# Graph attention in a four-layer network: the 0/1 matrices are compared on VectorE instead of GpSimd

## The chip, the cores and the metric

One core of a Trainium2 chip runs the whole program. The metric is the time of one execution on the device, in microseconds (us); lower is better. A measured time is the median of several executions. The profile is of one further execution and gives every instruction's start and duration.

## The reference, cut to what matters

Four layers follow each other: graph attention (GAT), a mixture-of-experts layer, a three-hop graph layer and a recurrent layer. The change touches only the attention over the edges of the first one: 6250 nodes with 256 features each, 100,000 edges sorted by destination, 4 heads of 64 channels.

```python
e = a_src[src] + a_dst[dst]                      # per edge and head
e = jnp.where(e > 0, e, NEG_SLOPE * e)
m = jax.ops.segment_max(e, dst, num_segments=n)
p = jnp.exp(e - m[dst])
denom = jax.ops.segment_sum(p, dst, num_segments=n)
alpha = p / jnp.maximum(denom[dst], 1e-16)
msg = alpha[:, :, None] * h_src[src]
out = jax.ops.segment_sum(msg, dst, num_segments=n).reshape(n, HC) + bias
```

## The kernel before, in words

The sorted edges lie in 832 tiles of 128 edges, and a tile's edges all end in one block of 128 destination nodes. `gat_attend` works through them in 104 groups of U = 8 tiles. For every tile a 128 x 128 matrix of zeros and ones says which edge (partition) ends in which node of the block (column). It is made by comparing a row of column numbers, `k.cols`, with each edge's place in the block, `local`. The fp32 matrix `S` multiplies the messages `M` on TensorE, which sums them per node (`product`, L1068). The bf16 copy `Sb` is used to find a running maximum (`spread_out`, L1037 and L1040) and is turned over on TensorE (`turn`, L1047).

Each engine runs its own list of instructions and waits on counters (semaphores). All lists are written in steps; step n has the end of group n and earlier stages of the groups n + 1, n + 2 and n + 3:

- GpSimd (POOL) compares the eight tiles of a group (`build`, L1001, eight instructions that write fp32 `S`), then issues the eight gathers that fetch rows of `table` for the group after it (`fetch`, L1007). Those are indirect DMAs into `G` (called all_X in the profile, since it lies in the room of X).
- ScalarE (ACT) takes the indices (`index`, L936 and L937), computes a correction (L962), copies part of the gathered rows (`collect`, L945), takes the turned matrices (`take_turned`, L954), casts `S` to bf16 (`halve`, L941), exponentiates (`weigh`, L958), scales the gathered rows of four tiles (`messages`, L968, 16 instructions), and last copies what the next step's `spread_out` multiplies (`sources`, AT, L949).
- TensorE (PE) goes through u = 0..7. It has `spread_out` for u = 0 and 1, then `ask` (L1055, L1057), `product` 0, `spread_out` 2, `turn`, `product` 1, `spread_out` 3, `product` 2 and so on. Here `spread_out` u may start only when VectorE has reduced `spread_out` u - 2 (counter `topped`), because two PSUM banks take turns.
- VectorE (DVE) begins a step with `bases` (L1166, L1167), two `message` instructions (L1209), with L1170 and L1173 between and behind them. Then come `reduce[0]` and `reduce[1]` (L1120, maxima of what `spread_out` made), `scale` (L1180), `into[0]` (L1220, adds `product` 0 to the sums), `whole` (L1189), `reduce[2]`, `into[1]` and so on up to `into[7]`. The small instructions for the logits lie between them; the last of those, `guard` (L1204), releases `weigh`. A chain for the maxima ends the step (L1136 to L1154). At every even step VectorE first loads 16 block numbers into registers (`blocks_of`), at the price of an idle engine before L1166.

What follows one step ahead of another on an engine is decided by this written order alone; nothing is scheduled by a tool.

Of the kernel before, what the change touches and what calls it, by code (L numbers as in the profile page):

```python
# [6 lines left out]
BF16 = mybir.dt.bfloat16  # L7
I32 = mybir.dt.int32
ACT = mybir.ActivationFunctionType
ALU = mybir.AluOpType  # L10
AXX = mybir.AxisListType.X

P = 128
# [13 lines left out]
U = 8  # L27
# [839 lines left out]
def gat_attend(nc, k, table, order, SRT, tile_block, QT, bigi, acc, room):  # L867
# [3 lines left out]
    with Phase(nc, "gs") as ph:  # L871
# [7 lines left out]
        local = ph.sb("local", [P, NS, U])  # L879
# [28 lines left out]
        indexed, turns, built, halved = ph.sem("indexed"), ph.sem("turns"), ph.sem("built"), ph.sem("halved")  # L908
# [18 lines left out]
        with ph.block() as block:  # L927
# [6 lines left out]
            def _(act):  # L934
# [4 lines left out]
                def halve(n, r):  # L939
                    act.wait_ge(built, n + 1)  # L940
                    nc.scalar.copy(Sb[:, r % 2], S[:, r]).then_inc(halved, 1)  # L941
# [30 lines left out]
                def step(n, r, i, there):  # L972
                    if there(0):
                        act.wait_ge(carried, (U - LATE) * (n + 1))
                        act.wait_ge(msgs, NPART * (n + 1))
                    if there(0) and there(4):
                        index(n + 4, r)
                    if there(0):
                        correct(n)
                    if there(3):  # L980
                        collect(n + 3, (r + 3) % NS, i + 1 if r else i)
                    if there(2):
                        take_turned(n + 2)
                    if there(3):
                        halve(n + 3, (r + 3) % NS)
                    if there(1):
                        weigh(n + 1, r + 1)
                        messages(n + 1, (r + 1) % NS)
                    if there(3):
                        sources(n + 3, (r + 3) % NS)  # L990
# [6 lines left out]
            def _(pool):  # L997
                def build(n, r):
                    pool.sem_inc(turns)
                    for u in range(U):  # L1000
                        last = nc.gpsimd.tensor_scalar(S[:, r, u], k.cols[:], local[:, r, u:u + 1], None, ALU.is_equal)  # L1001
                    last.then_inc(built, 1)

# [7 lines left out]
                for n in range(NS):  # L1011
                    pool.wait_ge(indexed, n + 1)
                    if n < 3:
                        build(n, n)
                    fetch(n, n)
                with pool.Fori(1, QUADS) as i:
                    for r in range(NS):
                        n = NS * i + r
                        pool.wait_ge(indexed, n + 1)
                        build(n - 1, (r - 1) % NS)  # L1020
                        fetch(n, r)
                pool.wait_ge(msgs, NPART * (GROUPS - NS + 1))
                build(GROUPS - 1, NS - 1)

            @block.tensor
            def _(pe):
# [4 lines left out]
                def spread_out(n, r, u):  # L1031
                    if u == 0:
                        pe.wait_ge(halved, n + 1)
                        pe.wait_ge(acopied, n + 1)
# [26 lines left out]
                def product(n, r, u):  # L1061
                    if u < LATE:
                        pe.wait_ge(msgs, n * NPART + next(j for j, (a, z) in enumerate(PARTS) if a <= u < z) + 1)
                    else:
                        pe.wait_ge(carried, n * (U - LATE) + u - LATE + 1)
# [33 lines left out]
            def _(dve):  # L1099
# [5 lines left out]
                ch.mark(nc.vector.tensor_copy(eye[:], k.ident[:]))  # L1105
                ch.mark(nc.vector.reduce_sum(picks[:], k.ident[0:TA, 0:TA].rearrange("p (u j h) -> p u h j", u=U, j=TERMS), AXX))
# [9 lines left out]
                dve.sem_inc(ready, 1)  # L1116

# [106 lines left out]
                def step(n, r, i, there):  # L1224
# [14 lines left out]
                    for j in range(1, NPART):  # L1239
                        if there(0):  # L1240
                            message(r, j)
                        if j == 1:
                            apart()
                    reduce[0]()
# [1330 lines left out]
```

## Time and profile before

| | |
|---|---|
| median of 3 executions | 17562.97 us |
| lowest and highest | 17558.74 and 17570.36 us |
| profiled execution, first to last instruction | 17545.4 us |
| the attention's edge part, `gat_attend` | 1254 to 2852 us of it, 1598 us |
| VectorE, GpSimd, TensorE, ScalarE busy in that part | 1329.62, 1312.56, 1204.22, 732.83 us |
| granted TensorE clock there, share of full speed | 0.80 |

The profiled execution's span is 17.6 us less than the median of the timed ones, which also hold what lies before the first and behind the last instruction. Busy time is a union over an engine's instructions. The edge part is 9% of the span; the recurrent layer, from about 7500 us on, is most of the rest.

### The profile page before, as it was taken

Reading aid. Unit: us, or ns where it says so; the run is one execution under the profiler, and the core shown is the slowest. Engines: PE = TensorE matmul, PEld = TensorE weight load, DVE = VectorE, ACT = ScalarE, POOL = GpSimd, SP = SyncE. Lnnn points to the kernel's source line nnn. Section 1 sums busy time; section 2 is a strip of 40 time slices with the busy share of each in tenths; the row PEclk is TensorE's granted clock in tenths of the full one; section 3 lists DMA queues with packets and bytes.
Section 4 is the critical chain, followed back from the end, with each engine's and each line's share of the span. In section 5 each row is a group of like instructions: output and inputs, shape, how many; then the busy total and the mean of one; then the engine's idle time right before and its main releaser. Section 6 shows DMA issues by size and latency. Waiting matters only on the chain. (4 is left out here: it accounts for less than half of the span.)

```text
span 17545.4 us, 683245 instructions
## 1 busy us (share of the span) xinstructions
PE 12730.7 (73%) x250869; PEld 10213.3 (58%) x250870; DVE 11697.3 (67%) x68713; ACT 5986.8 (34%) x41949; POOL 5631.1 (32%) x6174
## 2 busy tenths in 40 slices
PE   5247773399655656556888888888888888888887
PEld 3135552266444544445777777777777777777776
DVE  7368887322555454556777777777777777777777
ACT  0004442011100101003555555554555555555555
POOL 4778887666576575772000000000000000000000
PEclk6558886599877777775555555555555555555555
DMA  0102222111333333331000000000000000000000
GB/s 22 25 21 73 74 72 43 56 34 33 101 105 98 96 105 87 105 105 37 4 4 4 4 4 4 4 4 4 4 4 4 4 4 4 4 4 4 4 4 18
DMA packets 352412, 609.44 MB, mean 35 GB/s; under 512 B 157501, under 2 KB 232222, under 8 KB 348988
## 3 DMA queue, kind: packets, MB, share of 16 engines
q0 software_dynamic: 223104, 471.33, 10.4%
q1 hardware_dynamic: 126524, 100.27, 1.9%
q8 instruction: 1835, 30.06, 0.7%
q14 instruction: 949, 7.77, 0.1%
HBM read 508.72 MB, written 62.45 MB: 33 GB/s over the span
## 5 line engine op out<-in xcount | busy, mean ns | idle before, releaser
L2402 PE MATMUL lr_ZI<-ls_h,ls_V 128*128 128x1 f16 x150000 | 5006.8, 166 | 1669.7 <-DVE ls_h L2451 1412.8
L2402 PEld LDWEIGHTS lr_ZI<-ls_h,ls_V 128*128 128x128 f16 x150000 | 4487.3, 104 | 2677.0 <-DVE ls_h L2451 2640.4
L2419 ACT ACTIVATE ls_tg<-lr_ZI 128x2 f32<-128x2 f32 x12500 | 2150.0, 172 | 4626.5 <-PE lr_ZI L2402 4534.6
L2446 DVE TENSOR_TENSOR_SCAN lr_c<-ls_tg,ls_one_hc 128x2 f32<-128x2 f32 x12500 | 2118.1, 170 | 1441.0 <-ACT ls_tg L2419 1317.8
L2358 POOL COPY ls_HT<-ls_h 128x250 f32 x50 | 19.8, 395 | 9358.3 <-DVE ls_h L2456 9358.3
L2402 PE MATMUL lr_ZO<-ls_h,ls_V 128*128 128x1 f16 x75000 | 2865.0, 165 | 0.0
L671 PE MATMUL prop_sum<-prop_G,prop_S 128*128 128x256 f32 x4992 | 1830.4, 546 | 1369.9 <-DMA prop_G<-hop_table,prop_idx 1369.9
L657 POOL DMA_INDIRECT prop_G<-hop_table,prop_idx x2496 | 2368.3, 949 | 1057.3 <-issue 708.8
L2402 PEld LDWEIGHTS lr_ZO<-ls_h,ls_V 128*128 128x128 f16 x75000 | 2483.2, 104 | 0.0
L671 PEld LDWEIGHTS prop_sum<-prop_G,prop_S 128*128 128x128 f32 x4992 | 1403.9, 288 | 1796.3 <-issue 1486.1
L2451 DVE TENSOR_TENSOR ls_h<-ls_to 128x1 f16<-128x1 f32 x12500 | 2023.4, 162 | 479.1 <-ACT ls_to L2424 16.0
L2424 ACT ACTIVATE ls_to<-lr_c 128x1 f32<-128x1 f32 x12500 | 2102.5, 169 | 9.9 <-DVE lr_c L2446 1.0
L2422 ACT ACTIVATE ls_to<-lr_ZO 128x1 f32<-128x1 f32 x12500 | 2069.3, 171 | 0.0
L2455 DVE TENSOR_TENSOR_SCAN ls_h<-ls_to,ls_h 128x2 f16<-128x2 f32 x12500 | 1633.5, 162 | 25.7 <-issue 25.7
L694 DVE TENSOR_TENSOR gnn_agg<-gnn_agg,prop_sum 128x256 f32 x1664 | 694.9, 418 | 908.7 <-PE prop_sum L671 884.9
L2458 DVE TENSOR_TENSOR ls_one_hc<-ls_h,lr_c 128x1 f32<-128x1 f32 x6250 | 969.0, 155 | 220.0
L633 ACT CAST prop_idx<-gnn_SRT 128x8 int32 (+1 forms) x312 | 63.3, 203 | 2915.2 <-DMA prop_G<-hop_table,prop_idx 2903.7
L680 DVE TENSOR_SCALAR prop_S<-all_cols,prop_lw 128x128 f32<-128x128 f32 x2520 | 900.5, 358 | 165.6 <-issue 153.3
L2456 DVE TENSOR_TENSOR ls_h<-ls_to 128x2 f32<-128x2 f32 x6250 | 952.9, 152 | 7.2 <-issue 7.2
L2459 DVE TENSOR_TENSOR ls_one_hc<-ls_h,lr_c 128x1 f32<-128x1 f32 x6250 | 930.2, 149 | 0.0
L522 POOL DMA_INDIRECT sd_records<-sc_rec,sc_place x784 | 772.5, 985 | 440.7 <-issue 408.0
L1007 POOL DMA_INDIRECT all_X<-gat_table,gs_idx x832 | 825.3, 992 | 239.1 <-issue 239.1
(455 smaller groups left out, 13965.7 us busy)
## 6 DMA issues: line engine op xcount, KB each, us to landing
prop_G<-hop_table,prop_idx POOLq DMA_INDIRECT x2496, 2.7
mow_W<-in_L_ffn_W SPq DMA_DIRECT2D x16, 1024.0 KB, 10.8
moe_out<-me_Ys SPq DMA_DIRECT2D x108, 128.0 KB, 1.7
all_X<-gat_table,gs_idx POOLq DMA_INDIRECT x832, 2.8
hop_table<-ht_T SPq DMA_DIRECT2D x50, 256.0 KB, 2.1
sd_records<-sc_rec,sc_place POOLq DMA_INDIRECT x784
ss_records<-me_recs,me_places POOLq DMA_INDIRECT x540
gat_table<-gt_hs SPq DMA_DIRECT2D x50, 128.0 KB, 1.8
```

The costliest lines, as they stand in the source:

```text
L657: nc.gpsimd.indirect_dma_start(out=G[:, r, u, :], out_offset=None, in_=table[:, :], in_offset=bass.IndirectOffsetOnAxis(ap=idx[:, r, u:u + ...
L671: nc.tensor.matmul(ps[u][:, 0:D], S[:, r % 2, u, :], G[:, r, u, :], start=True, stop=True).then_inc(mm, 1)
L2402: mm = nc.tensor.matmul(place(hf, bank, col, 1), (V2 if part == "21" else V1)[:, q, ROWS.index(row), :], hx[:, prev, q, 1:2], start=False, ...
L2419: nc.scalar.activation(tg[:, s % 2, m, :], place(hf, m, col, 2), ACT.Tanh, scale=back).then_inc(gates[m], 1)
L2422: nc.scalar.activation(to[:, s % 2, m, 1:2], place(hf, KD + m, col, 1), ACT.Sigmoid, scale=back)
L2424: nc.scalar.activation(to[:, s % 2, m, 0:1], c[m][:, 1:2], ACT.Tanh, scale=0.5).then_inc(tanh_made[m], 1)
L2446: nc.vector.tensor_tensor_scan(c[m][:, 0:2], tg[:, e, m, :], one_hc[:, m, :], 1.0, ALU.mult, ALU.add).then_inc(cell[m], 1)
L2451: nc.vector.tensor_tensor(h1[:, r, m, 1:2], to[:, e, m, 1:2], to[:, e, m, 0:1], ALU.mult).then_inc(h1_made[m], 1)
L2455: nc.vector.tensor_tensor_scan(h2[:, r, m, :], to[:, e, m, :], h1[:, r, m, :], 1.0, ALU.mult, ALU.subtract).then_inc(h2_made[m], 1)
L2456: nc.vector.tensor_tensor(h[:, r, :], to[:, e, :, 1], to[:, e, :, 0], ALU.mult).then_inc(h_made, 1)
L2458: nc.vector.tensor_tensor(one_hc[:, 0, 1:2], h[:, r, 0:1], c[0][:, 1:2], ALU.mult)
L2459: nc.vector.tensor_tensor(one_hc[:, 1, 1:2], h[:, r, 1:2], c[1][:, 1:2], ALU.mult).then_inc(hc_made, 1)
```

## The change

`build` leaves GpSimd. VectorE now compares a whole group, 8 x 128 columns, with one `tensor_tensor` that reads bf16 column numbers and bf16 `local` and writes `Sb`. ScalarE's `halve` (fp32 to bf16) becomes `widen` (bf16 to fp32), of the same 1024 columns. The new VectorE instruction stands in step n for group n + 3, between `apart` (L1173) and `reduce[0]`. On ScalarE `take_turned` now comes ahead of `collect`. GpSimd keeps only the gathers.

```diff
-        local = ph.sb("local", [P, NS, U])
+        local, cols = ph.sb("local", [P, NS, U], BF16), ph.sb("cols", [P, P], BF16)
...
-                def halve(n, r):
+                def widen(n, r):
                     act.wait_ge(built, n + 1)
-                    nc.scalar.copy(Sb[:, r % 2], S[:, r]).then_inc(halved, 1)
+                    nc.scalar.copy(S[:, r], Sb[:, r % 2]).then_inc(widened, 1)
...
-                    if there(3):
-                        collect(n + 3, (r + 3) % NS, i + 1 if r else i)
                     if there(2):
                         take_turned(n + 2)
                     if there(3):
-                        halve(n + 3, (r + 3) % NS)
+                        collect(n + 3, (r + 3) % NS, i + 1 if r else i)
+                        widen(n + 3, (r + 3) % NS)
...
-                def build(n, r):
-                    pool.sem_inc(turns)
-                    for u in range(U):
-                        last = nc.gpsimd.tensor_scalar(S[:, r, u], k.cols[:], local[:, r, u:u + 1], None, ALU.is_equal)
-                    last.then_inc(built, 1)
-
...
                     for r in range(NS):
                         n = NS * i + r
                         pool.wait_ge(indexed, n + 1)
-                        build(n - 1, (r - 1) % NS)
                         fetch(n, r)
-                pool.wait_ge(msgs, NPART * (GROUPS - NS + 1))
-                build(GROUPS - 1, NS - 1)
...
                     if u == 0:
-                        pe.wait_ge(halved, n + 1)
+                        pe.wait_ge(built, n + 1)
                         pe.wait_ge(acopied, n + 1)
...
                 def product(n, r, u):
+                    if u == 0:
+                        pe.wait_ge(widened, n + 1)
...
+                def build(n, r, first):
+                    dve.wait_ge(indexed, n + 1)
+                    if not first:
+                        dve.wait_ge(widened, n - 1)
+                    nc.vector.tensor_tensor(Sb[:, r % 2], cols[:].unsqueeze(1).broadcast_to([P, U, P]),
+                                            local[:, r].unsqueeze(2).broadcast_to([P, U, P]), ALU.is_equal).then_inc(built, 1)
...
                         if j == 1:
                             apart()
+                    if there(3):
+                        build(n + 3, (r + 3) % NS, not there(1))
                     reduce[0]()
                     reduce[1]()
```

On VectorE this is the place in the middle of the steps, before the change; gs_gap is `apart`, gs_top the reductions, gat_acc `scale` and `into`.

```order
L1209 TENSOR_TENSOR gs_M<-all_X,gs_M 128x8x64
L52 REGISTER_ALU
L1173 TENSOR_TENSOR gs_gap<-gs_pair 128x4 [waits gs_pairs]
L1119 ISA
L1120 TENSOR_REDUCE gs_top<-gs_M 128x4 [waits gs_spread]
L1119 REGISTER_ALU
L1120 TENSOR_REDUCE gs_top<-gs_M 128x4 [waits gs_spread]
L1178 ISA [waits gs_corrected]
L1180 ISA [waits gs_added]
L1180 TENSOR_TENSOR gat_acc<-gat_acc,gs_corr 128x260
L1220 TENSOR_TENSOR gat_acc<-gat_acc,gs_O 128x260 [waits gs_scaled,gs_mm]
```

And this is the same place in the changed kernel, whose lines there have numbers that are lower by one or two.

```order
L1207 TENSOR_TENSOR gs_M<-all_X,gs_M 128x8x64
L52 REGISTER_ALU
L1171 TENSOR_TENSOR gs_gap<-gs_pair 128x4 [waits gs_pairs]
L1110 REGISTER_ALU
L1113 TENSOR_TENSOR gs_Sb<-gs_cols,gs_local 128x1024 [waits gs_widened,gs_indexed]
L1117 ISA
L1118 TENSOR_REDUCE gs_top<-gs_M 128x4 [waits gs_spread]
L1117 REGISTER_ALU
L1118 TENSOR_REDUCE gs_top<-gs_M 128x4 [waits gs_spread]
L1176 ISA [waits gs_corrected]
```

One instruction of 1024 columns, with waits on `widened` and `indexed`, has come between the messages and the first reduction.

On ScalarE this piece of the difference stands in the middle of the steps; hops0 is the counter of a group's gathers, gs_ST the turned matrices.

```order
 L937 COPY gs_idx<-edges_SRT 128x8
 L962 ACTIVATE gs_corr<-gs_gap 128x4 [waits gs_paired]
-L944 ISA
-L945 COPY gs_GA<-all_X 128x96 [waits hops0]
 L953 ISA
 L954 CAST gs_ST<-gs_T 128x512 [waits gs_trans]
 L953 REGISTER_ALU
 L954 CAST gs_ST<-gs_T 128x512 [waits gs_trans]
-L941 CAST gs_Sb<-gs_S 128x1024 [waits gs_built]
+L944 ISA
+L945 COPY gs_GA<-all_X 128x96 [waits hops0]
+L941 CAST gs_S<-gs_Sb 128x1024 [waits gs_built]
```

The copy that waits for the gathers has moved behind the two casts, and the cast of 1024 columns has turned round.

## Rows read from the trace of the kernel before

**Rows 1.** The page: the span.

```profile
span 17545.4 us, 683245 instructions
```

**Rows 2.** Windows, cut at every second step's L1166: busy time, clock, DMA.

```profile
core 0: us, PE busy (x) PEld busy (x) DVE busy (x) ACT busy (x) POOL busy (x), PEclk, DMA share, GB/s
1996.80:2025.50 28.70, 20.99 (x158) 13.88 (x155) 25.02 (x75) 14.05 (x50) 24.14 (x32) 0.87 0.28 72
2025.50:2055.40 29.90, 23.69 (x173) 16.09 (x172) 25.19 (x75) 14.08 (x50) 25.16 (x33) 0.78 0.28 75
...
sum 119.40, PE 92.39 PEld 61.98 DVE 100.72 ACT 56.35 POOL 100.78; mean PE 23.10 PEld 15.49 DVE 25.18 ACT 14.09 POOL 25.20
```

**Rows 3.** Groups by line, 1320 to 2820 us: busy, mean ns, idle before, releasers.

```profile
L1007 POOL DMA_INDIRECT all_X<-gat_table,gs_idx x798 | 790.4, 990 | 229.3 <-issue 229.3
L1001 POOL TENSOR_SCALAR gs_S<-all_cols,gs_local 128x128 f32<-128x128 f32 x800 | 468.0, 600 | 3.6 <-ACT gs_idx L937 0.5
...
L1220 DVE TENSOR_TENSOR gat_acc<-gat_acc,gs_O 128x260 f32 x804 | 334.6, 416 | 125.3 <-PE gs_O L1068 118.6
...
L1209 DVE TENSOR_TENSOR gs_M<-all_X,gs_M 128x512 f32<-128x512 f32 x202 | 138.0, 685 | 0.0
...
L941 ACT CAST gs_Sb<-gs_S 128x1024 bf16<-128x1024 f32 x100 | 104.6, 1046 | 155.7 <-POOL gs_S L1001 155.6
...
L1166 DVE TENSOR_TENSOR gs_pair<-gs_mine,gat_QT 128x4 f32<-128x4 f32 x101 | 16.4, 162 | 70.1 <-issue 70.1
```

**Rows 4.** Timeline of step 48: start, duration, instruction, [idle before, releaser].

```profile
2026.43 1.21 PE L1068 MATMUL gs_O<-gs_M,gs_S 128*128 128x260 f32 x2
...
2026.99 1.27 DVE L1120 TENSOR_REDUCE gs_top<-gs_M 128x4 f32<-128x512 f32 x2
...
2027.72 0.61 PE L1037 MATMUL gs_M<-gs_bigs,gs_Sb 128*128 128x512 bf16 x1
...
2029.40 1.18 PE L1068 MATMUL gs_O<-gs_M,gs_S 128*128 128x260 f32 x2
...
2030.73 0.42 DVE L1220 TENSOR_TENSOR gat_acc<-gat_acc,gs_O 128x260 f32 x1 [0.73 <-PE gs_O L1068]
...
2034.91 0.17 DVE L1204 TENSOR_SCALAR gs_e<-gs_e 128x32 f32<-128x32 f32 x1
```

**Rows 5.** Timeline of step 49, the next one.

```profile
2040.99 1.33 DVE L1120 TENSOR_REDUCE gs_top<-gs_M 128x4 f32<-128x512 f32 x2
...
2041.86 1.22 PE L1068 MATMUL gs_O<-gs_M,gs_S 128*128 128x260 f32 x2
...
2042.86 0.63 PE L1037 MATMUL gs_M<-gs_bigs,gs_Sb 128*128 128x512 bf16 x1
...
2043.11 0.42 DVE L1220 TENSOR_TENSOR gat_acc<-gat_acc,gs_O 128x260 f32 x1 [0.45 <-PE gs_O L1068]
...
2045.90 0.43 DVE L1220 TENSOR_TENSOR gat_acc<-gat_acc,gs_O 128x260 f32 x1 [1.25 <-PE gs_O L1068]
```

**Rows 6.** Timeline of step 47.

```profile
2011.67 1.28 DVE L1120 TENSOR_REDUCE gs_top<-gs_M 128x4 f32<-128x512 f32 x2
...
2012.81 0.63 PE L1037 MATMUL gs_M<-gs_bigs,gs_Sb 128*128 128x512 bf16 x1
```

**Rows 7.** Groups by line and shape on VectorE, 0 to 2900 us.

```profile
L247 DVE TENSOR_TENSOR ss_oh<-ssb_bins,ss_binrow 128x400 bf16<-128x400 f32 x197 | 108.9, 573 | 71.5 <-DVE ss_pos L343 29.9 <-PEq L251 29.1 <-PE ss_cnt L306 11.1
...
L1309 DVE TENSOR_TENSOR gf_XL<-gat_acc,gf_den 128x3200 f32<-128x3200 f32 x4 | 13.7, 3485 | 0.0
...
L1109 DVE CAST gs_pick<-gs_picks 96x4096 bf16<-96x4096 f32 x1 | 2.3, 2290 | 0.0
```

**Rows 8.** Timeline of the first steps.

```profile
1254.78 4.67 POOL L1001 TENSOR_SCALAR gs_S<-all_cols,gs_local 128x128 f32<-128x128 f32 x8 [12.54 <-ACT gs_idx L937]
...
1288.38 0.27 ACT L945 COPY gs_GA<-all_X 128x96 bf16<-128x96 bf16 x1 [13.93 <-DMA all_X<-gat_table,gs_idx]
...
1303.04 0.27 ACT L945 COPY gs_GA<-all_X 128x96 bf16<-128x96 bf16 x1 [12.31 <-DMA all_X<-gat_table,gs_idx]
```

More of the change, by code:

```diff
@@ L907, in gat_attend @@
         ready, primed, listed, mapped = ph.sem("ready"), ph.sem("primed"), ph.sem("listed"), ph.sem("mapped")
-        indexed, turns, built, halved = ph.sem("indexed"), ph.sem("turns"), ph.sem("built"), ph.sem("halved")
+        indexed, turns, built, widened = ph.sem("indexed"), ph.sem("turns"), ph.sem("built"), ph.sem("widened")
         collected, aturned, acopied, spread, topped = ph.sem("collected"), ph.sem("aturned"), ph.sem("acopied"), ph.sem("spread"), ph.sem("topped")
@@ L1012, in _ @@
                     pool.wait_ge(indexed, n + 1)
-                    if n < 3:
-                        build(n, n)
                     fetch(n, n)
@@ L1105, in _ @@
                 ch.mark(nc.vector.tensor_copy(eye[:], k.ident[:]))
+                ch.mark(nc.vector.tensor_copy(cols[:], k.cols[:]))
                 ch.mark(nc.vector.reduce_sum(picks[:], k.ident[0:TA, 0:TA].rearrange("p (u j h) -> p u h j", u=U, j=TERMS), AXX))
```

## The prediction, made before the changed kernel ran

> **What bounds the kernel now.** I read the edge part step by step, since nothing else changes. First the windows: eight steps take 119.4 us, 14.93 us each, and no engine is full; GpSimd and VectorE are both busy for 12.6 us of a step [rows 2]. Then the groups by line. GpSimd spends 8 x 0.60 us on compares and 8 x (0.99 + 0.29) us on gathers, the 0.29 being the "issue" idle of 229.3 us over 798 of them: 4.8 + 10.2 = 15.0 us, all of a step. It waits for nobody [rows 3]. So GpSimd looks like the bound, and a change that takes a third of its work away looks like a clear gain.
>
> VectorE's idle time argues against that. It is 2.3 us a step (14.93 - 12.59) [rows 2]: 1.25 us before L1220, nearly all for TensorE's products, and 0.70 us before L1166, which is the loading of block numbers and belongs to the engine itself [rows 3]. None of it is a wait for GpSimd. The only one who waits for a compare is ScalarE's cast L941, 1.56 us a step, and ScalarE is busy for only 7.0 us of a step [rows 2, 3]. So GpSimd keeps pace with the others but seldom holds them. The loop that sets the step runs through VectorE and TensorE: reduction 0 frees a PSUM bank, `spread_out` 2 fills it, then come `turn` and `product` 1, and `into[1]` waits for that. In step 48 reduction 0 ends at about 2027.6 (two take 1.27 us), `spread_out` 2 starts at 2027.72, `product` 1 at 2029.40, and VectorE, which was there 0.73 us early, goes on at 2030.73 [rows 4].
>
> **The change, part by part.**
>
> *GpSimd* loses 4.8 us a step. Nobody but ScalarE's cast sees it, so I price it at nothing in the steady state. Its gathers start as soon as the indices are there, which is when the messages are made (ahead of reduction 0, 1.5 us into step 48), and are through 10.2 us later. The copy that wants them comes in the next step. If GpSimd did hold the loop, this would be worth what the second rival below says.
>
> *VectorE gains one compare of 1024 columns a step.* No row has it. From 512 to 3200 columns two-input instructions go from 685 to 3485 ns, 1.04 ns a column, so 1024 columns take 685 + 512 x 1.04 = 1.22 us; 400 columns compared in the same way, with one value repeated along the row, take 573 ns and lie on that line [rows 3, 7]. The next instruction starts some 0.08 us before such a record ends (in step 48 two reductions of 0.68 us make 1.27), so it costs the engine 1.15 us. From below: a cast of 4096 columns takes 2290 ns, 0.56 ns a column, half as long [rows 7]; at that pace the compare costs 0.6 us. I take 1.15 us, because the row of 573 ns is the same operation, in the same layout, though with fp32 inputs.
>
> The Trainium skill's "VectorE: DVE Perf Modes", § Rules for kernel authors, says that tensor_tensor in bf16 gets twice the rate; its "Vector Engine (DVE) Microarchitecture Reference", § 5.1 Performance modes, says that one element read again and again in a two-source op of 2-byte operands ran at the single rate. No row here has such an instruction. By estimates from these pages the compare would cost 0.6 us by the first and 1.15 by the second.
>
> *How much of it lands on the loop.* The compare stands right ahead of reduction 0, so everything that hangs on reduction 0 moves back by 1.15 us, unless TensorE was late anyway.
> - Even steps (48): `product` 0 ends at 2027.64 and reduction 0 at about 2027.6; TensorE is ready when the bank is. With the compare, `spread_out` 2 starts at about 2028.8, and `into[1]` moves by the same: +1.05 us. Its wait of 0.73 us hides nothing, since it hangs on the same reduction [rows 4].
> - Odd steps (49): TensorE begins later there, because VectorE has no numbers to load first; `product` 0 ends at 2043.08, reduction 0 already at about 2041.65. `spread_out` 2 at 2042.86 is 1.2 us behind the reduction. The compare fits in, and the waits of 0.45 and 1.25 us shrink instead: +0.0 us [rows 5].
> - Odd steps with a fast start (47): reduction 0 at about 2012.3, `spread_out` 2 at 2012.81, so 0.5 us is covered and +0.65 us is left [rows 6].
>
> Of four pairs of steps one is like (46, 47), and three are like (48, 49). The mean is ((1.05 + 0.65) + 3 x (1.05 + 0)) / 8 = 0.61 us a step.
>
> *The granted clock.* The pair 46 and 47 has 0.87 of full speed and takes 28.7 us, the other three have 0.77 to 0.78 and take (119.4 - 28.7) / 3 = 30.2 us [rows 2]. TensorE now idles about 1 us more per even step. If the fast pairs vanish, a pair costs 30.2 + 1.05 = 31.3 us, 15.64 us a step, +0.71. I take 0.65 us, between the two.
>
> *ScalarE.* `widen` casts as many columns as `halve`, 1.05 us, and has nothing to wait for: the compare is through at about 2.7 us of a step (1.5 + 1.15), and ScalarE reaches the cast after `take_turned`. What must not wait is `weigh`, behind `guard`, and that ends at 2035.1, 9.6 us into step 48 [rows 4]; about 6 us lie between for 2.5 us of copies. `collect` moves behind `take_turned`; TensorE wants it only after `spread_out` 5. Nothing is charged. The new waits of VectorE (`indexed`, `widened`) are for things that were done a step before.
>
> *The start.* The second and third `collect` wait 13.9 and 12.3 us for gathers, at 1288.38 and 1303.04, because GpSimd compares ahead of each [rows 8]. Without the three compares of 4.7 us the gathers come 4.7, 9.4 and 14 us earlier. The reductions and the chains of these steps then set the pace; I take 10 us saved of 14. In the last three steps there is no compare, and nothing changes.
>
> **The sum** against the profiled execution's own 17545.4 us [rows 1]: 101 steps x 0.65 = +66, less 10, is +56 us. The median of the runs shown is 17.6 us above that span and takes the same difference: 17563 + 56 = 17619 us.
>
> **The rivals.**
>
> *1. GpSimd is the bound after all (faster).* For it: it never pauses. If its cadence is what makes TensorE late, the waits for products go with it. A step is then VectorE's 12.59 + 0.70 + about 0.15 + 1.15 = 14.6 us, 0.33 less than now: 101 x -0.33 - 10 = -43 us, 17520. It decides once the wait before L1220 falls from 1.25 to under 0.6 us a step. Against it: that wait hangs on reduction 0 in the timeline, and the compare comes ahead of that. Chance 0.12.
>
> *2. Little is left of it (no change).* Either the compare runs at the rate of the cast: even steps +0.5, odd ones 0, 101 x 0.25 - 10 = +15 us, 17578. That has 0.07. Or all pairs become as fast as the first: 28.7 + 1.7 = 30.4 us a pair, 15.2 us a step, 101 x 0.27 - 10 = +17 us, 17580. With the pairs that end in between, that has 0.15.
>
> *3. Full price (slower still).* The clock sinks further or the slack of the odd steps is used up, and each step takes the whole 1.15 us: 101 x 1.15 - 10 = +106 us, 17669. The same direction has a collision: VectorE's compare reads two operands in SBUF while GpSimd's gathers run. Today L1209 does that in each step and its mean is 685 ns, on the line of the others, so VectorE loses nothing that shows. If each compare waited out a whole gather of 0.99 us [rows 3], half of that landing on the loop, it would be +50 us on top of the forecast, 17669 too. Chance 0.12 together, 0.03 of it the collision.
>
> The Trainium skill's "SBUF — State Buffer" calls the port pair that VectorE and GpSimd share an exclusive lock, held for the whole instruction, and counts a VectorE op with two SBUF inputs against a GpSimd op that reads SBUF. By that rule the collision would be there; the rows of L1209 do not show it.
>
> **How the numbers follow.** The forecast, +40 to +80 us, has 0.54, and the rivals 0.12, 0.22 and 0.12. A measurement of this kernel tells about 0.2%, 35 us, from no change. Faster by more holds rival 1: 0.12. Slower by more holds the forecast and rival 3, less a little for forecasts that come out low: 0.64. The rest is 0.24. For 8 in 10 the range takes in rivals 2 and 3, with 20 us beyond the latter for its rough size, and stops short of rival 1's 17520: 17535 to 17690 us. The forecast's own range is 17600 to 17645.
>
> **What would show it.** In the profile after: a compare of about 1.22 us (0.69 would be the fast rate); GpSimd at about 10 us a step; ScalarE no longer waiting for gathers; even steps near 15.1 us and odd ones near 16, pairs of 31 us; the idle before L1220 still near 1 us a step; the first full step about 10 us earlier. The forecast is wrong if pairs of steps fall under 29.5 us, which is rival 1, or if the odd steps grow as much as the even ones, which is rival 3.

## The result, and the profile after

The changed kernel takes 17614.52 us (median of 7 executions, 17610.99 to 17618.51). The kernel before, run beside it on the same chip, takes 17560.69 us (7 executions, 17555.98 to 17570.36). The ratio is 1.003, with a 95% interval of 1.0019 to 1.004: 0.3%, or 54 us, slower. The prediction said 17619 us, and 17535 to 17690 as its range.

The page's span after, against [rows 1]:

```profile
span 17609.2 us, 682620 instructions
```

The edge part in one window, 1254 to 2912 us (it ends at 2909; before it ended at 2852):

```profile
core 0: us, PE busy (x) PEld busy (x) DVE busy (x) ACT busy (x) POOL busy (x), PEclk, DMA share, GB/s
1254.00:2912.00 1658.00, 1223.14 (x8424) 812.39 (x8424) 1437.60 (x3965) 725.18 (x2601) 794.78 (x832) 0.77 0.27 69
```

GpSimd went from 1312.56 busy us to 794.78, VectorE from 1329.62 to 1437.60. TensorE's granted clock is 0.77 of full speed where it was 0.80. Four steps (48 to 51), two windows cut at every second step's L1164, which is the L1166 of before:

```profile
2048.30:2078.81 30.51, 22.28 (x152) 14.79 (x151) 27.19 (x76) 13.87 (x50) 15.27 (x16) 0.78 0.27 71
2078.81:2109.97 31.16, 23.48 (x180) 15.88 (x177) 27.28 (x77) 13.95 (x50) 15.17 (x16) 0.78 0.27 70
```

Each pair holds about 2 us more of VectorE than before [rows 2]. Before, pairs of steps took 29.9, 30.6, 30.2 and 28.7 us by turns, and the last kind had a granted clock of 0.87 to 0.88 against 0.77 to 0.78 (twice 0.83) in the others. After, the pairs take 30.3 to 31.7 us and none has more than 0.78: the fast pair is gone. Over groups 10 to 100 the mean step went from 14.95 to 15.63 us: even steps from 14.01 to 15.14, odd ones from 15.88 to 16.12. That is +0.68 us a step.

Groups by line in the edge part, 1320 to 2880 us (columns as in [rows 3]; L1000 is the old L1007, L1218 the old L1220, L1207 the old L1209, L1164 the old L1166):

```profile
L1000 POOL DMA_INDIRECT all_X<-gat_table,gs_idx x789 | 750.6, 951 | 787.6 <-ACT gs_idx L937 564.5 <-issue 223.1
...
L1218 DVE TENSOR_TENSOR gat_acc<-gat_acc,gs_O 128x260 f32 x799 | 335.4, 420 | 93.0 <-PE gs_O L1058 81.7
...
L1207 DVE TENSOR_TENSOR gs_M<-all_X,gs_M 128x512 f32<-128x512 f32 x200 | 136.5, 686 | 0.0
L1113 DVE TENSOR_TENSOR gs_Sb<-gs_cols,gs_local 128x1024 bf16<-128x1024 bf16 x99 | 120.9, 1221 | 0.0
...
L941 ACT CAST gs_S<-gs_Sb 128x1024 f32<-128x1024 bf16 x99 | 104.6, 1057 | 0.0
...
L958 ACT ACTIVATE gs_M<-gs_e 128x32 f32<-128x32 f32 x100 | 26.0, 260 | 348.3 <-DVE gs_e L1202 348.3
...
L1164 DVE TENSOR_TENSOR gs_pair<-gs_mine,gat_QT 128x4 f32<-128x4 f32 x100 | 16.4, 164 | 70.1 <-issue 70.1
```

GpSimd, which never paused, now waits 5.6 us a step for the next indices. ScalarE's wait for GpSimd's compares, 155.7 us before L941, is gone, and so is its wait for gathers, 343.5 us before `collect`. This is `collect` in the kernel before, 1320 to 2820 us:

```profile
L945 ACT COPY gs_GA<-all_X 128x96 bf16<-128x96 bf16 x100 | 27.1, 271 | 343.5 <-DMA all_X<-gat_table,gs_idx 343.5
```

In their place ScalarE waits 348.3 us for VectorE's last logits (L1202), where it waited 51.5. VectorE still spends nearly 1 us a step before L1218 waiting for products. So the engine that was relieved is idle, and what the others wait for goes back to VectorE and TensorE. ScalarE is part of that loop: TensorE waits 2.9 us a step for its copy `sources` (L949) at the start of a step, and waited 3.0 before.

The timeline of step 48, an even one, shows the price on the path (columns as in [rows 4]):

```profile
2048.30 0.16 DVE L1164 TENSOR_TENSOR gs_pair<-gs_mine,gat_QT 128x4 f32<-128x4 f32 x1 [1.65 <-issue]
...
2049.80 1.22 DVE L1113 TENSOR_TENSOR gs_Sb<-gs_cols,gs_local 128x1024 bf16<-128x1024 bf16 x1
...
2050.94 1.28 DVE L1118 TENSOR_REDUCE gs_top<-gs_M 128x4 f32<-128x512 f32 x2
...
2051.68 0.10 PEld L1025 LDWEIGHTS gs_M<-gs_bigs,gs_Sb 128*128 128x128 bf16 x1 [1.99 <-DVE gs_top L1118]
2051.68 0.61 PE L1025 MATMUL gs_M<-gs_bigs,gs_Sb 128*128 128x512 bf16 x1 [1.25 <-DVE gs_top L1118]
...
2053.36 1.18 PE L1058 MATMUL gs_O<-gs_M,gs_S 128*128 128x260 f32 x2
...
2054.70 0.42 DVE L1218 TENSOR_TENSOR gat_acc<-gat_acc,gs_O 128x260 f32 x1 [0.74 <-PE gs_O L1058]
```

The reader is to see the two waits in the middle. TensorE stands 1.25 us idle until the first reduction (L1118) gives the bank back; in step 48 of the kernel before it had no wait there [rows 4]. Then L1218, which is `into[1]`, waits 0.74 us for the product, as it waited 0.73 before [rows 4]. The whole chain has moved. And step 49, an odd one:

```profile
2064.59 1.22 DVE L1113 TENSOR_TENSOR gs_Sb<-gs_cols,gs_local 128x1024 bf16<-128x1024 bf16 x1
...
2065.73 1.28 DVE L1118 TENSOR_REDUCE gs_top<-gs_M 128x4 f32<-128x512 f32 x2
...
2066.47 0.10 PEld L1025 LDWEIGHTS gs_M<-gs_bigs,gs_Sb 128*128 128x128 bf16 x1 [0.53 <-DVE gs_top L1118]
2066.47 0.63 PE L1025 MATMUL gs_M<-gs_bigs,gs_Sb 128*128 128x512 bf16 x1
...
2069.36 0.43 DVE L1218 TENSOR_TENSOR gat_acc<-gat_acc,gs_O 128x260 f32 x1 [0.61 <-PE gs_O L1058]
```

Here `into[1]` starts 6.3 us into the step (2069.36 less 2063.09), as before (6.4), and its wait has shrunk from 1.25 to 0.61 us [rows 5]: the compare took the place of waiting.

### The profile page after: what moved, and what is told of

Same layout as the page of the kernel before. It is cut to its first block and busy times, and to the rows that moved or that the text cites. A ratio compares the mean times of both kernels' runs of the same rounds, so it can differ in the third digit from the quotient of the medians.

```text
span 17609.2 us, 682620 instructions
## 1 busy us (share of the span) xinstructions
PE 12741.8 (72%) x250869; PEld 10217.3 (58%) x250870; DVE 11833.5 (67%) x68818; ACT 5988.7 (34%) x41949; POOL 5111.5 (29%) x5342
## 5 line engine op out<-in xcount | busy, mean ns | idle before, releaser
L1000 POOL DMA_INDIRECT all_X<-gat_table,gs_idx x832 | 794.8, 955 | 820.0 <-ACT gs_idx L937 570.5
```

## The experiments

The chips on which these ran take 19,400 to 19,600 us for the kernel before, not 17,560: what lies ahead of the recurrent layer is longer there (the edge part begins at about 1880 us instead of 1254), and in the steps of the edge part VectorE, TensorE and ScalarE stand idle for 2 to 4 us at a time. Runs with the same letter (e, f, g, h) ran on the same chip, beside the same runs of the kernel before. Each is compared with those, and totals of different chips are not set side by side. No variant was timed on a chip like the first. What does carry over is the time of an instruction after the start of its step, read before any of those idle stretches: for the kernel before `into[1]` of an even step starts at +5.26 us on the first chip and on these.

| run | us | before, same chip | ratio (95% interval) | mean step | `into[1]`, even and odd step |
|---|---|---|---|---|---|
| e1_relief_alone | 19589.41 | 19423.92 | 1.0084 (1.0065 to 1.0102) | 19.74 | +5.26, +5.40 |
| e2_gpsimd_load_back | 19738.61 | 19423.92 | 1.0159 (1.0141 to 1.0176) | 21.14 | +6.40, +6.40 |
| e3_compare_twice | 19661.54 | 19423.92 | 1.0123 (1.0105 to 1.0141) | 20.36 | +7.53, +7.53 |
| e4_compare_before_into1 | 19586.55 | 19423.92 | 1.0082 (1.0064 to 1.0099) | 19.63 | +5.57, +5.57 |
| f1_relief_alone | 19705.13 | 19596.77 | 1.005 (1.0033 to 1.0068) | 19.89 | +5.26, +5.40 |
| f3_compare_twice | 19773.47 | 19596.77 | 1.0088 (1.0071 to 1.0105) | 20.50 | +7.53, +7.53 |
| f4_compare_before_into1 | 19677.21 | 19596.77 | 1.004 (1.0027 to 1.0052) | 19.82 | +5.57, +5.57 |
| f5_compare_in_idle | 19700.60 | 19596.77 | 1.0049 (1.0031 to 1.0066) | 19.87 | +5.26, +5.57 |
| g1_before_again | 19441.05 | 19416.51 | one execution | 17.73 | +5.26, +6.48 |
| g2_after_again | 19649.86 | 19416.51 | 1.0116 (1.0087 to 1.0144) | 20.20 | +6.40, +6.07 |
| g3_eight_tensor_scalar | 19678.33 | 19416.51 | 1.0131 (1.0102 to 1.016) | 20.70 | +6.56, +6.56 |
| h5_idle_one_gather | 19139.60 | 19431.10 | 0.9849 (0.9833 to 0.9865) | 14.94 | +5.26, +6.42 |

Mean steps are of groups 10 to 100; the last column is the median over the steps of that kind. In odd steps of g1 and g2 it stands for a wide spread, 5.2 to 8.2 us and 5.6 to 6.5.

**Relief alone (e1, f1).** Against the kernel before, GpSimd compares one tile of eight. The kernel leaves out the other seven compares, which does not change what the other engines do.

```diff
-                def build(n, r):
+                def build(n, r, tiles=range(U), count=True):
                     pool.sem_inc(turns)
-                    for u in range(U):
+                    for u in tiles:
...
-                        build(n - 1, (r - 1) % NS)
+                        build(n - 1, (r - 1) % NS, range(1))
                         fetch(n, r)
```

> The kernel before, in which GpSimd compares only one tile of each group (all eight for the first four groups); the other seven tiles of S keep an older group's zeros and ones, so that part of the computation is left out. VectorE, ScalarE and TensorE do what they did. GpSimd drops from 15 to about 11 us a step. My theory (GpSimd keeps pace but holds nobody; the step is set by VectorE and TensorE) expects a step within 0.15 us of the 14.95 us of before, and a total within 15 us of it. The rival (GpSimd's cadence was the bound, and the changed kernel's compare used its relief up) expects steps of about 13.5 to 14.2 us, 80 to 150 us less in total.

> The same kernel as e1 (GpSimd compares one tile of eight in each group, the other seven tiles keep an older group's zeros and ones), for a chip on which the kernel before takes its 17560 us, since in the first run everything ran at 19420 us and all steps had idle stretches of 2 to 4 us that wait for nothing. Against the kernel before of the same call my theory expects within 15 us and steps of 14.9 us; the rival expects 80 to 150 us less.

It came out 165 and 108 us slower, which neither theory said. That GpSimd bounds the kernel (the first rival) is refuted on these chips: seven eighths of its compares are gone and nothing got faster. But "relief is worth nothing" is wrong there too. What the steps there spend their time on shows in the groups of the kernel before on such a chip (g1, 2000 to 3700 us):

```profile
L1120 DVE TENSOR_REDUCE gs_top<-gs_M 128x4 f32<-128x512 f32 x765 | 518.8, 685 | 224.9 <-remote 115.8 <-PE gs_M L1040 95.4 <-issue 9.7
L1220 DVE TENSOR_TENSOR gat_acc<-gat_acc,gs_O 128x260 f32 x767 | 322.0, 420 | 158.5 <-remote 73.8 <-PE gs_O L1068 65.6 <-issue 7.3
```

"remote" is a wait for which the profile has no event on this core. On the first chip no wait of the edge part's steps has it, neither before nor after; here it is 190 us in two groups.

**The load put back (e2).** The changed kernel, with eight GpSimd compares a step that nobody reads.

```diff
+                def build(n, first=False):
+                    if not first:
+                        pool.wait_ge(spared, n)
+                    pool.sem_inc(turns)
+                    for u in range(U):
+                        last = nc.gpsimd.tensor_scalar(spare[:, u], k.cols[:], k.part[:, 0:1], None, ALU.is_equal)
+                    last.then_inc(spared, 1)
...
                         pool.wait_ge(indexed, n + 1)
+                        build(n - 1)
                         fetch(n, r)
```

> The changed kernel, in which GpSimd again issues eight compares of 128 columns ahead of each group's gathers, into a spare tile that nobody reads (column numbers against the partition number). My theory expects steps of 15.6 us, as in the changed kernel, and only the start to lose its gain: the first full step about 12 us later, 12 us more in total, 17627 us. The rival (GpSimd's relief is worth a good part of a microsecond a step) expects 30 us and more above the changed kernel, and ScalarE waiting for gathers again in every step.

The run has the longest steps of all, 21.14 us, and the 12 us that I expected are missed by far. The changed kernel itself did not run on this chip, but e3 did, which is the changed kernel with a second compare on VectorE, and e2 takes 77 us more than e3. Unless a second compare makes a kernel faster, the load on GpSimd costs here what the rival said, 30 us and more. The rival's other sign is missing: ScalarE waits for gathers in no step (0.0 us before its `collect`). Nor is GpSimd short of time, for it still waits 5.9 us a step for indices (563.5 us in 2000 to 4000 us). What has moved is the gathers, which begin 7.7 us into a step, behind the compares, instead of 2.84. The offset of `into[1]` is the changed kernel's, +6.40: within the step the extra GpSimd work delays nothing up to there, and the loss lies behind it. Why it is there is not shown.

**The compare twice (e3, f3).**

```diff
+                    nc.vector.tensor_tensor(spare[:, r % 2], cols[:].unsqueeze(1).broadcast_to([P, U, P]),
+                                            local[:, r].unsqueeze(2).broadcast_to([P, U, P]), ALU.is_equal)
                     nc.vector.tensor_tensor(Sb[:, r % 2], cols[:].unsqueeze(1).broadcast_to([P, U, P]),
```

> The changed kernel with the compare issued twice, the first time into a spare tile. In the changed kernel spread_out 2 follows right behind reduction 0 in even and in odd steps alike, so the slack of the odd steps should be used up: my theory expects the whole 1.15 us in both, 15.63 + 1.15 = 16.8 us a step and 101 x 1.15 = 116 us more in total, 17730 us. If odd steps still covered part of it, the total would rise by 60 to 90 us only. If the compares fought with the gathers, the record of a compare would be longer than 1.22 us and the rise over 120 us.

> The same kernel as e3 (compare issued twice on VectorE). Where the kernel before takes 17560 us, my theory expects 17730 us, the whole 1.15 us in even and odd steps. In the first run reduction 0 stood at 3.78 us of each step and into[1] at 7.53 us, against 2.64 and 6.40 us in the changed kernel: the second compare moved both by 1.13 us in each step, so the total should follow where nothing else stalls.

The second compare moves `into[1]` to +7.53 us in both kinds of step. In even steps of the changed kernel it stands at +6.40 on both chips where it ran, so the second one is paid in full, 1.13 us. In odd steps the comparison says less: on these chips they have hardly any slack to use up, since with no compare at all `into[1]` comes at +5.40 there (e1) and not at about +6.4 as on the first chip. That the price goes through reduction 0 is borne out in both; that the first compare used up the slack of the odd steps of the first chip is not tested by this run. Against relief alone on the same chip the two compares cost 72 us (e3 less e1) and 68 us (f3 less f1), some 0.7 us a step for 2.3 us of VectorE. The idle stretches take up the rest: those of over 0.9 us on VectorE sum to 2.3 us a step in e3 and to 4.1 in e1.

One step of e3 also shows what happens when a compare and a gather meet, which the changed kernel avoids (there the compare is through 2.7 us into a step and the first gather starts at 2.84):

```profile
2875.75 1.22 DVE L1114 TENSOR_TENSOR gs_spare<-gs_cols,gs_local 128x1024 bf16<-128x1024 bf16 x1
2876.89 1.22 DVE L1116 TENSOR_TENSOR gs_Sb<-gs_cols,gs_local 128x1024 bf16<-128x1024 bf16 x1
...
2877.09 1.84 POOL L1001 DMA_INDIRECT all_X<-gat_table,gs_idx  x1 [9.87 <-ACT gs_idx L938]
2879.92 0.94 POOL L1001 DMA_INDIRECT all_X<-gat_table,gs_idx  x1 [0.99 <-issue]
```

The compare keeps its 1.22 us, but the gather instruction that starts beside it takes 1.84 us instead of 0.95. It is so in each of the 92 steps between groups 8 and 100, of e3 and of f3 (1.83 us in the mean).

**The compare moved ahead of `into[1]` (e4, f4).** It stands behind `reduce[2]`, where VectorE would wait for the product.

```diff
-                    if there(3):
-                        build(n + 3, (r + 3) % NS, not there(1))
                     reduce[0]()
                     reduce[1]()
...
                     reduce[2]()
+                    if there(3):
+                        build(n + 3, (r + 3) % NS, not there(1))
                     into[1]()
```

> The changed kernel with the compare moved from ahead of reduction 0 to ahead of into[1], where VectorE waits 0.74 us (even steps) or, in the kernel before, 1.25 us (odd steps) for TensorE's product 1. My theory (the price comes from the place, because all that hangs on reduction 0 moves back) expects even steps 0.4 us and odd steps 0.0 us longer than before: about 15.15 us a step, and with the 12 us gained at the start 101 x 0.2 - 12 = +8 us against before, 17570 us. The rival (VectorE is simply out of time, wherever the compare stands) expects the 17615 us of the changed kernel.

> The same kernel as e4 (compare ahead of into[1]). In the first run into[1] stood at 5.57 us of each step with no wait ahead of it, against 5.27 or 6.43 us before the change and 6.40 us after it. Where the kernel before takes 17560 us, my theory expects 15.1 us a step and about 17570 us; the rival, that VectorE's time counts wherever it is spent, 17615 us.

`into[1]` starts at +5.57 us with no wait, where the kernel before has +5.26 with 0.74 us of it: the compare costs 0.31 us there in even steps, and 0.17 in odd ones against relief alone (+5.40). The total is that of relief alone (19586.55 and 19589.41 us) or a little less (19677.21 and 19705.13): in this place the VectorE compare adds nothing that these runs can tell. The 17570 us that I expected could not be read, since no chip took 17560 us for the kernel before. The timeline of one step of e4 shows what the idle stretches look like:

```profile
2729.34 0.39 PE L1028 MATMUL gs_M<-gs_AT,gs_pick 96*128 96x128 bf16 x4
2729.57 0.66 PE L1058 MATMUL gs_O<-gs_M,gs_S 128*128 128x260 f32 x2
2729.83 0.95 POOL L1000 DMA_INDIRECT all_X<-gat_table,gs_idx  x1 [0.30 <-issue]
2731.08 0.95 POOL L1000 DMA_INDIRECT all_X<-gat_table,gs_idx  x1 [0.30 <-issue]
2731.92 0.69 DVE L1118 TENSOR_REDUCE gs_top<-gs_M 128x4 f32<-128x512 f32 x1 [2.82 <-remote]
...
2732.67 0.39 PE L1025 MATMUL gs_M<-gs_bigs,gs_Sb 128*128 128x512 bf16 x1 [2.45 <-DVE gs_top L1118]
```

The matmuls that the reduction reads (L1028) end at 2729.73. The reduction starts at 2731.92, over 2 us after its input was there, and TensorE then waits for it. GpSimd goes on issuing gathers throughout.

**The compare in the idle of the register loads (f5).** In even steps it goes ahead of `blocks_of`, in odd ones it stays ahead of `into[1]`.

```diff
+                    if there(3) and r % 2 == 0:
+                        build(n + 3, (r + 3) % NS, not there(1))
                     if there(0) and r % 2 == 0:
                         held[0] = blocks_of(nc, mybir.EngineType.DVE, tile_block, n, 2)
...
-                    if there(3):
+                    if there(3) and r % 2:
                         build(n + 3, (r + 3) % NS, not there(1))
                     into[1]()
```

> The changed kernel with the compare put where VectorE's engine is idle: in even steps at the very start, ahead of the loading of block numbers (1.2 to 1.65 us in which the engine has nothing to do), in odd steps ahead of into[1] (a wait of 0.8 to 1.25 us before the change). If place is what counts, even steps cost nothing more than before and odd ones 0 to 0.3 us, and the start keeps its gain of 12 us: 17550 to 17565 us where before takes 17560. If the engine has to be empty before the loading begins, even steps grow by 1.15 us and the total is 17605 us or more.

The offsets of even steps are those of the kernel before, +5.26 us with a wait of 0.74. They count from L1164, though, behind the compare. Ahead of L1164 VectorE was idle for 1.40 us in the mean; now the compare and what idle time is left around it take 1.59, so the compare of 1.22 us costs 0.19 us every second step there. The total equals that of relief alone again (19700.60 and 19705.13 us).

**Both kernels again (g1, g2), and eight `tensor_scalar` (g3).**

> The kernel before, unchanged, as a control: in the two calls so far it took 19424 and 19597 us, 11% more than in the run that the prediction started from, and I have no trace of it there. If it is again near 19500 us, its steps should be about 19 us, with idle stretches of 2 to 4 us on VectorE that wait for nothing the profile shows, while reduction 0 and into[1] stand where they stood (1.51 us, and 5.3 or 6.4 us into a step). If it takes 17560 us, its trace should be that of the first run.

> The changed kernel as a control for the same chip. Where the kernel before takes 17560 us, 17615 us. Where it takes about 19500 us, odd steps start faster than they did (into[1] at 5.4 instead of 6.4 us in the kernels with the compare elsewhere or absent), so nothing covers the compare in them: my theory then expects nearly the whole 1.13 us in both kinds of steps, 100 us or more over before and between the two other versions with a compare (moved: 80 to 160 us over before; twice: 177 to 238 us over).

> The changed kernel, with eight tensor_scalar compares of 128 columns (bf16 in and out, the edge's place as a per-partition fp32 scalar) in the place of the one of 1024. If a one-source bf16 compare runs at the rate of the casts or faster, eight take 8 x 0.11 = 0.9 us from start to start and the step is 0.2 to 0.3 us shorter than in the changed kernel: 20 to 30 us less than it in the same call. If they run at one column a cycle, 8 x 0.21 = 1.7 us and 50 to 60 us more. If such compares wait for GpSimd's gathers, some records are lengthened by up to 1 us, and it is slower still.

The change costs 233 us on this chip, 1.2%, where it cost 54 us on the first. I had expected 100 us or more, and steps of about 19 us for g1, where they are 17.73. I had also expected less than the compare twice costs; that took 177 us on one chip and 238 on another, so these runs leave it open. Odd steps did start faster in g2 (+6.07), as expected, but the step grew by 2.47 us, twice what the compare itself can cost; the rest is in the idle stretches. First GpSimd in g1, 2000 to 3700 us, then VectorE's reductions and GpSimd in g2, 2000 to 3900 us:

```profile
L1007 POOL DMA_INDIRECT all_X<-gat_table,gs_idx x768 | 757.6, 986 | 220.7 <-issue 220.7
L1001 POOL TENSOR_SCALAR gs_S<-all_cols,gs_local 128x128 f32<-128x128 f32 x762 | 456.1, 612 | 262.8 <-ACT gs_idx L937 257.6 <-issue 4.0
```

```profile
L1118 DVE TENSOR_REDUCE gs_top<-gs_M 128x4 f32<-128x512 f32 x751 | 507.9, 687 | 369.2 <-remote 247.3 <-PE gs_M L1028 103.2 <-issue 12.7
...
L1000 POOL DMA_INDIRECT all_X<-gat_table,gs_idx x752 | 716.0, 952 | 1185.0 <-ACT gs_idx L937 971.8 <-issue 213.2
```

VectorE's idle stretches of over 0.9 us, without those of the register loads, sum to 2.6 us a step in g1 and to 3.7 in g2. On the first chip it was 0.5 before and 0.1 after, all of it waits for TensorE's products. Those on the slower chips end 4 to 12 us after a burst of gathers has begun.

Eight `tensor_scalar` over 128 bf16 columns have records of 251 ns and cost 1.29 us from start to start, the single `tensor_tensor` 1.13. That lies between the 0.9 and 1.7 us that I gave, and `into[1]` moves by the difference, to +6.56. The run takes 28 us more than g2, not 20 to 30 less; the two spreads overlap.

```profile
L1114 DVE TENSOR_SCALAR gs_Sb<-gs_cols,gs_local 128x128 bf16<-128x128 bf16 x776 | 134.6, 251 | 0.0
```

**One gather of eight (h5).** f5, and from the fifth group on GpSimd issues one gather instead of eight. The kernel leaves out the other seven, whose tiles keep old rows.

```diff
-                    act.wait_ge(got[r], before + i * (16 * U) + 16 * U)
+                    act.wait_ge(got[r], before + i * 16 + 16 * U)
...
-                        fetch(n, r)
+                        fetch(n, r, 1)
```

> The kernel of f5 (compare at the start of even steps and ahead of into[1] in odd ones), which from the fifth group on gathers only one tile of eight; the other seven keep the rows of an older group, so that part of the work is left out. Two questions. First, where the idle stretches of 2 to 4 us that wait for nothing come from: on the chips that take 19400 us or more they end 4 to 12 us after a burst of gathers began, so if gathers in flight cause them they should nearly go, from 3.8 us a step to under 1; if not, steps stay at 19.8 us. Second, what the place of the compare is worth without them: my theory expects 14.9 to 15.1 us a step, as in the kernel before on the first chip (14.95) and half a microsecond and more under the changed kernel there (15.63); the rival, that VectorE's time counts wherever it is spent, expects 15.6 us and more. In total about 480 us under f5 on such a chip, or 17550 us on one like the first.

Everything stays in place but the gathers, and the idle stretches are gone to the last one. The window over the steps, of f5 and then of h5:

```profile
1980.00:3920.00 1940.00, 1307.87 (x7785) 827.22 (x7909) 1363.11 (x3714) 684.98 (x2447) 753.37 (x779) 0.68 0.21 55
```

```profile
1980.00:3479.00 1499.00, 1149.48 (x8070) 774.93 (x8069) 1367.17 (x3809) 700.38 (x2503) 108.90 (x97) 0.80 0.03 9
```

and VectorE's two waiting groups, of f5 and of h5:

```profile
L1118 DVE TENSOR_REDUCE gs_top<-gs_M 128x4 f32<-128x512 f32 x782 | 528.3, 686 | 332.3 <-remote 286.0 <-PE gs_M L1028 34.7 <-issue 5.0
L1218 DVE TENSOR_TENSOR gat_acc<-gat_acc,gs_O 128x260 f32 x781 | 328.2, 420 | 204.8 <-remote 107.1 <-PE gs_O L1058 75.3 <-issue 10.5
```

```profile
L1119 DVE TENSOR_REDUCE gs_top<-gs_M 128x4 f32<-128x512 f32 x782 | 527.9, 683 | 10.0 <-PE gs_M L1029 6.0
L1219 DVE TENSOR_TENSOR gat_acc<-gat_acc,gs_O 128x260 f32 x782 | 326.5, 418 | 70.3 <-PE gs_O L1059 58.1
```

The step falls from 19.87 to 14.94 us. That is the step of the kernel before on the first chip, 14.95, although VectorE does the compares here. Even the pairs of steps agree: 29.8, 30.7, 30.2 and 28.7 us by turns, the last at a granted clock of 0.87. This suggests that in these two places the compare costs next to nothing. It does not show it, since the kernel before with one gather of eight was not run, and gathers could cost something on the first chip too. The timeline shows where the compare goes at the start of an even step:

```profile
2654.99 1.22 DVE L1114 TENSOR_TENSOR gs_Sb<-gs_cols,gs_local 128x1024 bf16<-128x1024 bf16 x1 [0.38 <-issue]
...
2656.45 0.16 DVE L1165 TENSOR_TENSOR gs_pair<-gs_mine,gat_QT 128x4 f32<-128x4 f32 x1 [0.24 <-issue]
...
2661.71 0.42 DVE L1219 TENSOR_TENSOR gat_acc<-gat_acc,gs_O 128x260 f32 x1 [0.74 <-PE gs_O L1059]
```

Where VectorE was idle for 1.65 us before L1164, it now is for 0.38 and 0.24 us, with the compare of 1.22 us between, 1.84 us in all: most of the compare runs while the registers are loaded, and about 0.2 us of it is paid, as in f5. In odd steps `into[1]` comes at +6.42 us, within 0.05 us of the kernel before (+6.37), and its wait has shrunk to 0.12: the compare fills it.

## Why the prediction was right, step by step

- *What bounds the kernel.* Right for the chip it was made for, as far as the two traces can show it; no variant ran there. GpSimd lost 518 us of work in the edge part and nothing became faster in the steady state. One reading was incomplete: L941 was not the only instruction that GpSimd held up. `collect` waited 343.5 us in the same steps, 3.4 us a step, for gathers that GpSimd issues behind its compares. Both are ScalarE's, and ScalarE had the room, so the price of nothing stood. And the 0.70 us a step before L1166 was taken for VectorE's own, where f5 shows that a compare fits into most of it. The first rival would have needed the wait before `into` under 0.6 us a step; it is 0.93.
- *The compare's price.* Predicted as a record of 1.22 us and 1.15 us on the engine; it is 1218 to 1226 ns, and 1.135 us from start to start in the median. bf16 on both sides brought no faster rate. The rule of the Trainium skill's "Vector Engine (DVE) Microarchitecture Reference", § 5.1 Performance modes, for an element that is read again and again held here, with 1221 ns. The twofold rate in the Trainium skill's "VectorE: DVE Perf Modes", § Rules for kernel authors, stands there for dense step-1 operands, and each element of `local` is read 128 times over. So it was not put to the test here, and the prediction's 0.6 us by that page left its condition out.
- *How much lands on the loop.* Even steps: predicted +1.05, measured +1.12 on the mean, and `into[1]` from +5.26 to +6.40. Odd steps: predicted 0 for three of four and +0.65 for the fourth, which is +0.16 on the mean, measured +0.24. Up to `into[1]` of an odd step the prediction held (+6.35 after, +6.37 before).
- *The granted clock.* Pairs of steps separate its part from the loop's. The three kinds of pairs with the lower clock took 30.3 us on the mean before, and after the change a pair takes 31.25: +0.98, where +1.05 was predicted. The fast kind, 28.7 us at 0.87, was to become 30.4 and is gone: that is +2.5 instead of +1.7. So the price in the loop was right, and what came on top of its 0.61 us is that the fast pairs vanished. The prediction had that case, 15.64 us a step and +0.71, and took a middle of 0.65; measured are 15.63 and +0.68. That the middle came so close is luck in part; both of its ends lie inside the forecast's range.
- *ScalarE.* Right: L941 waits 0.0 us in the steady state, and over the whole edge part `collect` waits for gathers 3 times, 14.6 us, where it was 104 times, 389.1 us; `weigh` waits for VectorE, not the other way round.
- *The start.* Predicted 10 us; the first full step begins at 1298.1 instead of 1310.1, 12.0 us earlier.

```profile
1280.62 0.27 ACT L945 COPY gs_GA<-all_X 128x96 bf16<-128x96 bf16 x1 [0.77 <-DMA all_X<-gat_table,gs_idx]
...
1291.10 0.27 ACT L945 COPY gs_GA<-all_X 128x96 bf16<-128x96 bf16 x1 [0.74 <-DMA all_X<-gat_table,gs_idx]
...
1298.10 0.16 DVE L1164 TENSOR_TENSOR gs_pair<-gs_mine,gat_QT 128x4 f32<-128x4 f32 x1 [1.62 <-issue]
```

  The waits of 13.9 and 12.3 us for gathers [rows 8] are 0.8 and 0.7 us here.
- *The sum.* 101 x 0.68 - 12 = +57 us, and the edge part ends 57.7 us later. Behind it, where nothing was changed, the profiled execution took 6 us more, so its span grew by 63.8; the medians differ by 54.
- *The collision* of a compare with the gathers had no chance to occur. The prediction let the gathers start 1.5 us into a step, beside the compare; they start at 2.84 us, when it is through. No compare and no message of the steady state runs beside a gather instruction in the changed kernel, so its longest record, 1226 ns, says nothing on this. In e3 they do meet, and the price falls on the other side: the compare keeps its 1.22 us and the gather takes 1.83.
- *Where it would have been wrong.* "GpSimd's relief is priced at nothing" does not hold everywhere. On the other chips the relief from seven eighths of the compares cost 108 to 165 us, and the whole change 1.2%, and putting the load back on the changed kernel did not help either but cost more (e2, 77 us over e3). The time there is set by idle stretches during the gathers. The prediction had no such term and could not read it from the first chip's trace.

What stays open: h5 shows that the idle stretches need most of the gathers, but it takes away their traffic, their descriptors and GpSimd's time with them together, so it doesn't say which. Why they are so much larger on some chips, and why every version that gathers all tiles has longer steps there than the kernel before, is not shown either. GpSimd's pauses for indices are longer in all of them (5.9 to 11 us a step against 2.7 in g1), but their length does not order the steps: e2 pauses least of them, 5.9 us, and has the longest steps. The placement of f5 was timed only where these stretches dominate; on the first chip it should, by an estimate from its offsets and h5, give back most of the 0.68 us a step, but that wasn't measured. No version that does the whole work beat the kernel before.

## What to carry to other kernels

Before work is moved off a busy engine, ask who waits for it: GpSimd was busy all of the step and still held nobody but two instructions of ScalarE with room to spare. On the engine that takes the work, the place counts more than the length. The same compare moves what follows by 1.13 us ahead of the reduction that frees a PSUM bank (less where TensorE is late anyway), by 0.2 to 0.3 us in front of an addition that waits for a product, and by 0.2 us ahead of register loads that leave the engine idle. And a kernel whose steps run beside indirect gathers should be timed on more than one chip.

## What the runs showed of the hardware that was not expected

- VectorE is idle for 1.2 or 1.65 us before L1164 while 16 numbers are loaded into registers. A compare of 1.22 us written ahead of the loads ran inside most of that time: idle, compare and idle take 1.84 us where the idle time was 1.65 (1.59 and 1.40 in the mean).
- A gather instruction of GpSimd that starts while VectorE's two-input compare runs takes 1.83 us instead of 0.95 (e3 and f3, in every step). The compare keeps its 1.22 us, also when a gather was running before it (e4, 1216 ns).
- The same program takes 17,560 us on one chip and 19,400 to 19,600 on others. The products of the recurrent layer, whose stretch moves only 4 GB/s, take about 9,354 and 9,380 us from first to last, so the difference lies ahead of them.
- On the slower chips instructions whose inputs are ready start 2 to 3 us late while gathers are issued (2.82 us "remote" before L1118 in e4). With one gather of eight left there is no such stretch, and the step is 14.94 us instead of 19.87.
- Less work on GpSimd made the kernel slower there: 1.0084 and 1.005 with one compare of eight left. More work on it made the changed kernel slower too: e2 takes 77 us more than e3.
